# One graph network kernel: the order of the attention steps, a compare moved to ScalarE, and the zeroing of a dense table begun one stage earlier

## The chip, the core and the metric

The kernel runs on one core of one Trainium2 chip. The metric is the time on the device in microseconds (us), the median of the runs shown; lower is better. The engines of the core are TensorE (PE in the rows, PEld its weight loads), VectorE (DVE), ScalarE (ACT), GpSimd (POOL) and SyncE (SP). They run in parallel and wait for each other through semaphores. DMAs are issued from SP's and from POOL's queue and carried by 16 DMA engines.

## What is computed

A graph of 6,250 nodes with 256 features and 100,000 edges sorted by destination goes through an attention layer and then through three SAGE layers:

```
h = relu(layernorm(x));  feat = h @ W_n                    # 6250 x 256, 8 heads of 32
el, er = feat . attn_l, feat . attn_r                      # 6250 x 8 x 4 kinds
e = sum over kinds of (el[src] + er[dst] + e_pro @ attn_m) * mask / 3
e = leaky(e);  p = exp(e - segment_max(e, dst)[dst])
x = x + segment_sum(feat[src] * p, dst) / segment_sum(p, dst)
h = relu(layernorm(x))
3 times: h = l2norm(mean over edges of relu(h @ pW + pb)[src] @ lW + lb + h @ rW), silu between
out = x + layernorm(h) * ln_w + ln_b
```

The kernel treats destinations below 1536 by a dense adjacency matrix (sources by 1536 destinations, fp32) in DRAM: it is zeroed in 49 blocks of 128 rows, and then 199 scattered writes of 128 numbers each put the edge counts in.

## The kernel before

The program is unrolled by hand and has four stages.

- `setup` loads weights and indices.
- `node_features` goes over the 49 blocks of nodes in 7 groups of 7. Per group SP loads x (L373 under `load`), DVE takes the moments and ACT normalises (`norm`), PE transposes and multiplies (`project`), DVE copies the result into `table_rows` and `right_rows`, and POOL stores them (two DMAs) and waits until they have landed before it frees the rows.
- `attention` (L1365 to L1806) goes over the edges in 112 chunks of 7 tiles of 128 edges. Everything of chunk c has its step c in each engine's own order.
- `layers` are the three SAGE layers, among them the products with the dense adjacency matrix.

In `attention`, POOL gathers the 7 tiles of rows of chunk c (`gather_chunk`, 7 indirect DMAs, L499) into a ring of 5 chunks, once the sums of chunk c-5 are done (`summed`); from chunk BUILD_FROM = 54 on it adds BUILD_EACH = 4 of the scattered writes (`place_edges`, L508) behind each chunk's gathers until all 199 are out. SP loads the edges 5 chunks ahead, stores the window sums and, in steps 1 to 49, issues one block of the zeroing (L1501).

PE in step c: `left_of(c+1)` (L1535), `sum_tiles(c-1)` for tiles 0 to 3 (L1565), `to_heads(c)` (L1545 to L1548), `kinds_of(c+2)` (L1523 and 14 products at L1528), `to_edges(c)` (L1555), `sum_tiles(c-1)` for tiles 4 to 6 and the carried-over window (L1573, sets `summed`), and then a product or a transpose of a node block.

DVE in step c: `score_of(c+1)` (L1632 to L1644), `other_side(c+2)` (L1620, compares destinations with partitions and writes `one_hotT`), `run_maxima(c)` (two scans, L1652 and L1655, wait for `to_heads(c)`), every second step one of 18 pieces of counting double edges (`count_piece`, L528, L536, L539), node work (`node_norm`, `node`, `biased`), `below_max(c)` (L1663, waits for `to_edges(c)`), `shifting(c)`, and `weigh(c)` (L1678, after ACT's exponential). The 49 node blocks have slots in 49 of the steps (`slot_at`, at distances of 2 or 3); `node(n)` runs in the slot's step, `node_norm(n)` one step later, `biased(n)` four steps later.

ACT in step c: `own_side(c)` (7 absolute differences at L1775 and one relu over 128x896 at L1779), `soften(c)` (the exponentials), `normed`, `keep(c-1)` (waits for `summed`), and the node blocks' `turned` and `positive`.

## Time and profile before

| | us |
|---|---|
| median of 3 runs | 4472.72 (4471.12 to 4472.92) |
| the profiled execution | 4519.99 |
| its span, first to last instruction | 4518.3 |
| `node_features`, 60.6 to 172.9 | 112.3 |
| attention, first to last `weigh` | 1507.1 |
| `layers`, from 1772.3 | 2746.0 |

The profile is of one execution that took 1.06% longer than the median. A row of a view by groups gives line, engine, operation, output<-input, shapes and count, then busy us and mean ns of one, then the idle time of the engine just before them and what ended it. A row of the timeline gives start, length, engine, line, operation, and in brackets the idle time before it. Views by stretches give busy time and count of each engine, the granted TensorE clock (1.00 is 2.4 GHz, 0.50 is 1.2 GHz), the share of the DMA engines' time and GB/s.

### The profile page before, as it was taken

Reading aid. Unit: us, or ns where it says so; the run is one execution under the profiler, and the core shown is the slowest. Engines: PE = TensorE matmul, PEld = TensorE weight load, DVE = VectorE, ACT = ScalarE, POOL = GpSimd, SP = SyncE. Lnnn points to the kernel's source line nnn. Section 1 sums busy time; section 2 is a strip of 40 time slices with the busy share of each in tenths; the row PEclk is TensorE's granted clock in tenths of the full one; section 3 lists DMA queues with packets and bytes.
Section 4 is the critical chain, followed back from the end, with each engine's and each line's share of the span. In section 5 each row is a group of like instructions: output and inputs, shape, how many; then the busy total and the mean of one; then the engine's idle time right before and its main releaser. Section 6 shows DMA issues by size and latency. Waiting matters only on the chain.

```text
span 4518.3 us, 47445 instructions
## 1 busy us (share of the span) xinstructions
PE 3383.0 (75%) x15322; PEld 2402.7 (53%) x15322; DVE 1793.9 (40%) x5198; ACT 721.0 (16%) x2002; POOL 2672.4 (59%) x2803
## 2 busy tenths in 40 slices
PE   3477777766666676789888876898888768887875
PEld 2366556545444553456555554565555445555555
DVE  3267776544444454123232231232322313433425
ACT  1233333222222231001011110010101100000000
POOL 0355555666666653666666646666666466666663
PEclk9788889777878788799899887999999878888887
DMA  4477778544444453455555434555554345555552
GB/s 126 140 227 227 235 238 251 150 126 126 127 126 126 126 152 117 149 172 170 172 168 176 137 118 141 173 174 169 175 166 147 104 151 178 186 178 170 179 161 79
DMA packets 435311, 724.66 MB, mean 160 GB/s; under 512 B 110349, under 2 KB 260309, under 8 KB 435060
## 3 DMA queue, kind: packets, MB, share of 16 engines
q0 software_dynamic: 132272, 362.86, 28.4%
q1 hardware_dynamic: 300880, 356.54, 24.4%
q8 instruction: 124, 2.03, 0.2%
q10 hardware_dynamic: 1908, 2.19, 0.1%
q14 instruction: 127, 1.04, 0.1%
HBM read 626.59 MB, written 94.70 MB: 160 GB/s over the span
## 4 chain that ended last, share of the span: by engine, by line
PE 39%; issue 10%; another core or an unknown queue 6%; DVE 5%; ACT 0%; DMA 0%; SPq 0%; DVEq 0%
PE ps L1191 17%; PE ps L1132 16%; PE ps L1167 3%; PE ps L1157 2%; DVE attention_work L1223 1%; DVE block_cube L699 1%; DVE block_inv_norm L701 1%; DVE block_o L1254 1%; PE ps L593 0%; DVE attention_work L1245 0%; DVE root L1246 0%; DVE block_inv_norm L696 0%; DVE block_half L693 0%; DVE block_bn L651 0%
## 5 line engine op out<-in xcount | busy, mean ns | idle before, releaser
L1068 POOL DMA_INDIRECT ring<-message_table,src_index x1797 | 1704.6, 949 | 1058.9 <-issue 497.7
L1191 PE MATMUL ps<-attention_work,ring 128*128 128x128 f32 (+1 forms) x7188 | 1055.5, 295 | 392.8 <-issue 390.2
L1191 PEld LDWEIGHTS ps<-attention_work,ring 128*128 128x128 f32 x7188 | 980.5, 202 | 515.2 <-issue 493.6
L499 POOL DMA_INDIRECT ring<-attention_table,src_index x784 | 756.4, 965 | 529.1 <-issue 207.3
L1132 PE MATMUL ps<-attention_work 128*128 128x512 f32 x1764 | 856.0, 627 | 66.2 <-issue 40.1
L1565 PE MATMUL ps<-ring,one_hot 128*128 128x265 f32 x1568 | 544.7, 502 | 417.7 <-issue 417.7
L1565 PEld LDWEIGHTS ps<-ring,one_hot 128*128 128x128 f32 x1568 | 362.0, 244 | 530.7 <-issue 452.6
L1132 PEld LDWEIGHTS ps<-attention_work 128*128 128x128 f32 x1764 | 349.1, 204 | 492.1 <-issue 465.6
L1254 DVE SCALAR_TENSOR_TENSOR block_o<-ps,inv_deg,root 128x256 f32<-128x256 f32 x147 | 71.0, 483 | 872.6 <-remote 738.8
L1223 DVE TENSOR_TENSOR attention_work<-ps,attention_work 128x1024 f32<-128x1024 f32 (+1 forms) x225 | 273.4, 1216 | 361.7 <-DMA attention_work<-run_flags 359.9
L1235 DVE TENSOR_TENSOR block_aT<-ps,attention_work 128x256 f32<-128x256 f32 x111 | 47.1, 424 | 517.9 <-DMA attention_work<-run_flags 350.2
L1167 PE MATMUL ps<-w_pr,block_hT 128*128 128x512 f32 x392 | 231.7, 714 | 16.0 <-issue 14.1
L1775 ACT ACTIVATE one_hot<-iota_row,dst_rel 128x128 f32<-128x128 f32 x784 | 240.1, 391 | 19.3 <-PEq L146 19.3
L508 POOL DMA_INDIRECT dense_adjacency<-times,cell x199 | 197.0, 990 | 60.6 <-issue 60.6
L1678 DVE TENSOR_TENSOR ring<-ring,ps 128x1792 f32<-128x1792 f32 x112 | 226.4, 2022 | 3.1 <-ACT ps L1764 0.3
L1528 PEld LDWEIGHTS ps<-attention_work 128*128 128x128 f32 x1568 | 205.8, 202 | 2.1 <-DVE attention_work L1620 0.7
L1764 ACT ACTIVATE ps<-attention_work 128x56 f32<-128x56 f32 x112 | 24.8, 221 | 1079.2 <-DVE attention_work L1663 1050.8
L1528 PE MATMUL ps<-attention_work 128*128 128x32 f32 x1568 | 194.7, 278 | 0.1
L1652 DVE TENSOR_TENSOR_SCAN ps<-attention_work,ps 56x224 f32<-56x224 f32 x112 | 69.5, 621 | 264.5 <-PE ps L1548 125.0
L1348 ACT ACTIVATE attention_work<-block_o,block_shift,block_inv_norm 128x256 f32<-128x256 f32 x49 | 29.5, 601 | 840.2 <-DVE block_shift L1280 511.0
L1663 DVE TENSOR_TENSOR attention_work<-attention_work,ps 128x56 f32<-128x56 f32 x112 | 23.8, 212 | 332.6 <-DMA edge_keys<-ring 323.7
L1325 ACT ACTIVATE block_hT<-ps 128x256 f32<-128x256 f32 x98 | 37.7, 384 | 712.7 <-remote 376.6
(165 smaller groups left out, 3012.3 us busy)
## 6 DMA issues: line engine op xcount, KB each, us to landing
attention_work<-dense_adjacency SPq DMA_DIRECT2D x441, 256.0 KB
attention_work<-message_table SPq DMA_DIRECT2D x441, 128.0 KB
attention_work<-in_dst_edges SPq DMA_DIRECT2D x112, 448.0 KB
dense_adjacency<-root SPq DMA_DIRECT2D x49, 768.0 KB
ring<-message_table,src_index POOLq DMA_INDIRECT x1797
attention_sums<-sums_out SPq DMA_DIRECT2D x112, 132.5 KB
ring<-attention_table,src_index POOLq DMA_INDIRECT x784
message_table<-attention_work SPq DMA_DIRECT2D x98, 128.0 KB
```

The costliest lines, as they stand in the source:

```text
L499: pool.indirect_dma_start(m.ring[:, k, t, 0:cols], None, table, bass.IndirectOffsetOnAxis(ap=m.src[:, at:at + 1], axis=0)).then_inc(s[f"ro ...
L508: pool.indirect_dma_start(cells, bass.IndirectOffsetOnAxis(ap=m.cell[:, j:j + 1], axis=0), m.times[:, j:j + 1], None, bounds_check=BLOCKS ...
L1068: pool.indirect_dma_start(m.wide_ring[:, k, j, :], None, m.tables[w.l], bass.IndirectOffsetOnAxis(ap=m.src[:, t:t + 1], axis=0)).then_inc( ...
L1132: last = nc.tensor.matmul(m.ps[:, 2 + half, :], m.m_rows[:, k, half * P:(half + 1) * P], m.a_rows[:, k, :], start=(j == 0), stop=(j == BLO ...
L1167: last = nc.tensor.matmul(m.ps[:, 5, :], m.b_hT[:, k * P:(k + 1) * P], m.w_pr[:, w.l + 1, k, :], start=(k == 0), stop=(k == 1))
L1191: last = nc.tensor.matmul(group_sums(m, w.bank(g), (q % 2 * WIDTH + j) * PITCH, cols)[:, k, :], m.wide_ring[:, u % RING, j, k * P:(k + 1) ...
L1223: nc.vector.tensor_tensor(hot, m.iota_ps[:, None, :].to_broadcast([P, len(tiles), P]), m.dst_at[:, tiles[0]:tiles[-1] + 1][:, ::-1][:, :, ...
L1254: nc.vector.scalar_tensor_tensor(m.b_o[:], m.ps[:, 0, 0:D], m.inv_deg[:, n:n + 1], m.root[:, n, :], ALU.mult, ALU.add).then_inc(s["o"].sem, 1)
L1528: last = nc.tensor.matmul(m.ps[:, 0, t * 32:(t + 1) * 32], m.one_hotT[:, t * P:(t + 1) * P], m.right[:, k, :], start=False, stop=False)
L1565: last = nc.tensor.matmul(m.ps[:, 6 + parity, 0:SUMC], m.one_hot[:, parity, t, :], m.ring[:, k, t, 0:SUMC], start=(t == 0), stop=(c == 0 a ...
L1678: nc.vector.tensor_tensor(ring_heads[k][:, :, :, 0:HD], ring_heads[k][:, :, :, 0:HD], weights[:, :, :, None].to_broadcast([P, TILES, HEADS ...
L1775: last = nc.scalar.activation(m.one_hot[:, c % 2, t, :], m.iota_row[:], ACT.Abs, bias=m.dst_rel[:, at:at + 1], scale=-1.0)
```

## The change

- PE: the sums of chunk c-1 are split in three: tiles 0 and 1 before `to_heads(c)`, tiles 2 to 4 between `to_heads(c)` and `to_edges(c)`, tiles 5 and 6 after `kinds_of(c+2)`, which itself moves behind `to_edges(c)`.
- `other_side` moves from DVE (one compare) to ACT (an absolute difference and a relu, each over 128x896), ahead of `own_side` in the step.
- DVE: the counting pieces run in steps 1 to 18, one in each, before `run_maxima`; `node` and `node_norm` are cut in four parts, of which two go before `run_maxima`, one after it, and one (the moments) between `below_max` and `weigh`.
- Zeroing: 28 of the 49 blocks are issued in `node_features`, four behind each group's load of x on SP's queue, and the stage ends only when they have landed; the other 21 go out in attention steps 0 to 20.
- POOL: the 199 scattered writes are spread evenly behind the gathers of chunks 23 to 111 (2 or 3 each) instead of 4 behind each from 54 on.

```diff
-BEFORE = 4
-COUNT_FROM = 2
+COUNT_FROM = 1
-ZERO_FROM, BUILD_FROM, BUILD_EACH = 1, 54, 4
+ZERO_EACH = 4
+ZERO_HEAD = ZERO_EACH * GROUPS
+BUILD_FROM = 23
+def zero_block(eng, m, rows):
+    rows = rows.rearrange("o p n -> (o p) n") if len(rows.shape) == 3 else rows
+    return eng.dma_start(rows.rearrange("p (k n) -> p k n", n=ZEROS),
+                         m.zero_rows[:, None, :].to_broadcast([P, DENSE // ZEROS, ZEROS]))
@@ node_features, sync: load
                 group_dma(sp, x_g, g, m.x_in[:, b]).then_inc(s[f"x{b}"], 16)
+                if isinstance(g, int):
+                    sp.wait_ge(s["zeros"].sem, 1)
+                for k in range(ZERO_EACH):
+                    zero_block(sp, m, m.adj_groups[bass.ds(g, 1), k]).then_inc(s["zeroed"], 16)
             groups(sp, load, lambda g, b: None)
+            sp.wait_ge(s["zeroed"], 16 * ZERO_HEAD)
@@ attention, gpsimd
-                if c >= BUILD_FROM and placed < OWN:
+                if c >= BUILD_FROM:
                     if not placed:
                         pool.wait_ge(s["counted"].sem, COUNTED + 2)
-                        pool.wait_ge(s["zeroed"], 16 * BLOCKS)
-                    last = min(OWN, placed + BUILD_EACH)
+                        pool.wait_ge(s["zeroed"], 16 * (BLOCKS - ZERO_HEAD))
+                    last = OWN * (c + 1 - BUILD_FROM) // (CHUNKS - BUILD_FROM)
                     place_edges(pool, m, s, range(placed, last))
@@ attention, tensor
-                    sum_tiles(c - 1, range(BEFORE))
+                    sum_tiles(c - 1, range(2))
                 if c < CHUNKS:
                     to_heads(c)
+                if 0 < c <= CHUNKS:
+                    sum_tiles(c - 1, range(2, 5))
+                if c < CHUNKS:
+                    to_edges(c)
                 if c + 2 < CHUNKS:
                     kinds_of(c + 2)
-                if c < CHUNKS:
-                    to_edges(c)
                 if 0 < c <= CHUNKS:
-                    sum_tiles(c - 1, range(BEFORE, TILES))
+                    sum_tiles(c - 1, range(5, TILES))
@@ attention, vector, the step
                     score_of(c + 1)
-                if c + 2 < CHUNKS:
-                    other_side(c + 2)
+                if COUNT_FROM <= c < COUNT_FROM + 3 * RUN_PARTS:
+                    count_piece(nc, dve, m, s, c - COUNT_FROM)
+                elif c == COUNT_FROM + 3 * RUN_PARTS:
+                    place_cells(nc, dve, m, s)
+                for n in at_step(c, 1):
+                    node_scale(n)
+                for n in at_step(c, 0):
+                    node_weights(n)
                 if c < CHUNKS:
                     run_maxima(c)
-                if c >= COUNT_FROM and (c - COUNT_FROM) % 2 == 0:
...
-                for n in at_step(c, 1):
-                    node_norm(n)
                 for n in at_step(c, 0):
-                    node(n)
+                    node_sum(n)
...
                     biased(n)
                 if c < CHUNKS:
                     below_max(c)
                     if c:
                         shifting(c)
+                for n in at_step(c, 0):
+                    node_moments(n)
+                if c < CHUNKS:
                     weigh(c)
@@ attention, scalar
+            def other_side(c):
+                edges_in(act, c)
+                if c:
+                    act.wait_ge(s["right"].sem, s["right"].done(c - 1))
+                nc.scalar.activation(m.one_hotT, m.dst_bc[:, c % EDGES, :], ACT.Abs, bias=m.window_p[:, c:c + 1],
+                                     scale=-1.0).then_inc(s["distance"].sem, 1)
+                act.wait_ge(s["distance"].sem, s["distance"].done(c))
+                nc.scalar.activation(m.one_hotT, m.one_hotT, ACT.Relu, bias=1.0, scale=-1.0).then_inc(s["oht"].sem, 1)
+            other_side(0)
+            other_side(1)
             for c in range(steps):
+                if c + 2 < CHUNKS:
+                    other_side(c + 2)
                 if c < CHUNKS:
                     own_side(c)
```

## Rows read from the trace of the kernel before

**Rows 1.** The page: busy time of each engine, and the clock in 40 slices.
```profile
PE 3383.0 (75%) x15322; PEld 2402.7 (53%) x15322; DVE 1793.9 (40%) x5198; ACT 721.0 (16%) x2002; POOL 2672.4 (59%) x2803
PEclk9788889777878788799899887999999878888887
```

**Rows 2.** Stretches: length, then PE, PEld, DVE, ACT, POOL, clock, DMA share, GB/s.
```profile
60.60:172.90 112.30, 74.56 (x294) 52.67 (x294) 53.73 (x260) 39.79 (x64) 13.42 (x14) 0.91 0.41 131
690.90:811.30 120.40, 95.72 (x481) 73.73 (x481) 80.24 (x207) 46.02 (x137) 72.97 (x78) 0.94 0.83 254
811.30:1618.50 807.20, 515.75 (x2178) 391.75 (x2178) 373.00 (x988) 206.18 (x616) 531.66 (x550) 0.79 0.46 126
```

**Rows 3.** Stretches counted by L1678 alone, one per chunk: length, busy (count).
```profile
240.20:449.00 208.80, 36.39 (x18) 0.88 0.77 234
449.00:690.80 241.80, 40.43 (x20) 0.86 0.77 235
690.80:811.20 120.40, 22.24 (x11) 0.94 0.83 254
811.20:1618.40 807.20, 101.08 (x50) 0.79 0.46 126
```

**Rows 4.** Timeline of POOL, the end of one chunk and the next.
```profile
1033.09 0.97 POOL L508 DMA_INDIRECT dense_adjacency<-times,cell  x1 [0.31 <-issue]
1034.37 0.97 POOL L508 DMA_INDIRECT dense_adjacency<-times,cell  x1 [0.30 <-issue]
1037.79 0.98 POOL L499 DMA_INDIRECT ring<-attention_table,src_index  x1 [2.45 <-remote]
```

**Rows 5.** Timeline of PE and DVE in the same chunk.
```profile
1031.19 0.27 PE L1555 MATMUL ps<-ident,attention_work 56*128 56x56 f32 x1
1032.83 0.61 PE L1573 MATMUL ps<-sums_out,shift_mat 128*128 128x265 f32 x2
1037.45 0.21 DVE L1663 TENSOR_TENSOR attention_work<-attention_work,ps 128x56 f32<-128x56 f32 x1 [4.63 <-DMA edge_keys<-ring]
```

**Rows 6.** Timeline of POOL at the gathers' starts of chunks 9, 23 and 111.
```profile
283.73 0.94 POOL L499 DMA_INDIRECT ring<-attention_table,src_index  x1 [1.97 <-PE ps L1573]
...
448.91 0.95 POOL L499 DMA_INDIRECT ring<-attention_table,src_index  x1 [2.26 <-PE ps L1573]
...
1699.77 0.94 POOL L499 DMA_INDIRECT ring<-attention_table,src_index  x1 [1.94 <-remote]
```

**Rows 7.** DVE's groups from 240.2 to 690.8, 38 chunks.
```profile
L1620 DVE TENSOR_TENSOR attention_work<-attention_work,ps 128x896 f32<-128x896 int32 x38 | 40.9, 1076 | 0.0
L536 DVE TENSOR_REDUCE root<-root 128x199 f32<-128x1592 f32 x12 | 35.3, 2944 | 0.0
L1652 DVE TENSOR_TENSOR_SCAN ps<-attention_work,ps 56x224 f32<-56x224 f32 x38 | 23.6, 621 | 84.0 <-PE ps L1548 40.3 <-issue 25.6 <-remote 18.0
L528 DVE TENSOR_TENSOR root<-keys 128x1976 f32<-128x1976 f32 x6 | 13.1, 2182 | 0.0
L539 DVE TENSOR_TENSOR root<-root 128x199 f32<-128x199 f32 x10 | 3.7, 367 | 0.3
```

**Rows 8.** ACT's group of the relu, same stretch.
```profile
L1779 ACT ACTIVATE one_hot<-one_hot 128x896 f32<-128x896 f32 x38 | 36.2, 951 | 1.2
```

**Rows 9.** DMA in 40 slices of 0.65 us, two groups of `node_features`, 101 to 127.
```profile
DMA  0008999960000949991000099999500005599900
GB/s 0 0 0 321 357 357 270 353 151 0 0 0 6 54 147 373 388 384 60 0 0 0 0 350 372 350 262 349 126 0 0 0 24 106 165 386 388 318 25 0
```

**Rows 10.** GB/s in 40 slices, 253 to 258, a zeroing block issued at 253.76.
```profile
GB/s 344 258 201 401 267 305 362 257 249 202 319 302 400 253 393 374 284 250 231 226 164 244 111 240 348 381 349 393 393 442 377 393 410 377 442 377 431 398 387 333
```

**Rows 11.** Timeline, the first counting piece beside a gather.
```profile
246.10 2.18 DVE L528 TENSOR_TENSOR root<-keys 128x1976 f32<-128x1976 f32 x1
246.48 2.63 POOL L499 DMA_INDIRECT ring<-attention_table,src_index  x1 [0.30 <-issue]
```

41 lines of the change are left out of this document (14 added, 27 removed).

## The prediction, made before the changed kernel had run

> **What bounds the kernel now.** I read the page first. No engine is busy throughout: PE has 75%, POOL 59%, DVE 40%, ACT 16% [rows 1]. So the question is which chain sets the pace in each stage, and the view by stretches comes next. The change touches `node_features` (112.3 us, DMA share 0.41) and the attention [rows 2]; `layers` is neither shortened nor fed with other data, and I carry its 2746 us over unchanged.
>
> Inside the attention one DVE instruction, `weigh` at L1678, marks each chunk. Counting it by stretches gives the pace [rows 3]: 208.8 / 18 = 11.60 us per chunk at first, 241.8 / 20 = 12.09 after that, 120.4 / 11 = 10.95 where the counting pieces are over, and 807.2 / 50 = 16.14 in the stretch where POOL adds four scattered writes per chunk. The reader is to see that half of the attention's time lies in the last figure, and that PE, DVE and ACT are all idler there (PE 515.8 of 807.2 us, clock down to 0.79) than in the stretch before it (95.7 of 120.4, clock 0.94) [rows 2]. Something on POOL's side sets the pace.
>
> POOL's timeline shows what: each indirect DMA takes 0.95 to 1.0 us and the next starts 0.30 us later, and between two chunks there is a gap, here 2.45 us [rows 4]. A gather is thus worth 1.25 us and a scattered write 1.28; 7 x 1.25 + 4 x 1.29 = 13.9 us, and 16.14 - 13.9 leaves 2.2 us for the gap. Without the writes the same gap is 1.9 to 2.3 [rows 6], so POOL's floor for a bare chunk is 7 x 1.25 + 2.0 = 10.8 us, just under the 10.95 of [rows 3]. **POOL's queue is the floor of both kinds of chunk.** The gap is odd: the semaphore it waits for was set by L1573 at 1033.4, and DVE's L1663 stood 4.6 us although L1555 had ended at 1031.5 [rows 5]. Both go on about 2 us after POOL's last DMA. I cannot say from the trace what holds them; I take the gap as a price per chunk.
>
> **Part 1, the scattered writes spread.** POOL does the same 784 gathers and 199 writes. What can be gained is only the time in which it now stands still for the other engines outside the build. From the start of chunk 23's gather (448.91) to that of chunk 111 (1699.77) the kernel takes 1250.9 us [rows 6]. Afterwards all 88 intervals hold 199 / 89 = 2.24 writes on average: 16.14 - 1.76 x 1.29 = 13.86 us each, 1220 us in all. That is **-31 us**. It holds if the other engines need less than 13.5 us per chunk; they need 10.95 or less now. The lower bound takes the gap at 1.97 instead of 2.2 [rows 6]: -31 - 88 x 0.23 = -51. The upper bound lets four in ten steps, those with the most node work, run over by 0.5 us: -13.
>
> **Part 2, the counting, now in every one of steps 1 to 18.** A piece is 2.9 us of DVE ((13.1 + 35.3 + 3.7) / 18) [rows 7]. What one costs the pace now: 38 chunks took 450.6 us against 38 x 10.95 = 416, so 34.5 / 18 = 1.9 us each; the rest falls in waits. Twice the density over 18 steps gives 10.95 + 1.9 = 12.9 us per chunk. Against that `other_side` leaves DVE, 1.08 us per chunk [rows 7], and the pieces stand where DVE now waits for `to_heads`, 84.0 / 38 = 2.2 us per chunk [rows 7]. But that wait shrinks, for `to_heads` has only two tiles of sums ahead of it, and `kinds_of` now lies between `to_edges(c)` and `left_of(c+2)`, so the next score comes later. The two roughly cancel. I take 12.4, half a microsecond less than the plain sum for the compare. Against 11.60 that is 18 x 0.8 = **+14 us**. Bounds: the piece hidden whole, 11.2 (-7); not hidden at all, 13.9 (+41).
>
> **Part 3, the rest of the reordering.** Where POOL is the floor, a shorter chain on PE or DVE buys nothing, so from step 19 on I cost the new order of sums, `kinds_of` and node parts at zero. What hides it is POOL's 13.9 us per chunk. `summed` is set about 1.5 us later than before (2.1 us of `kinds_of` stand ahead of it in place of one tile and a half of sums), which POOL's wait would feel if the step were over 12 us; that is inside part 1's upper bound. ACT gets two instructions like L1779, 2 x 0.95 = 1.9 us per chunk [rows 8], on top of 46.0 / 11 = 4.2 [rows 2]. ACT now waits for `right` there, with `own_side` and `soften` queued behind it, and `weigh` waits for `soften`. 6.1 us of work in a step of 10.8 or more leaves room: 0, with 1 us at the start, where nothing covers ACT's first two. If the cover went, the price would be 1.9 us per chunk.
>
> **Part 4, zeroing in `node_features`.** A block is 786 KB, four are 3.15 MB. A group's own traffic is 0.92 MB of x and 1.18 MB of stores, in two bursts of about 3 and 4 us at 350 GB/s, with pauses between them; two groups fill 26 us [rows 9]. While a zeroing block moves, the DMA engines carry some 400 GB/s [rows 10], so four take 7.9 us. 7 + 7.9 = 14.9 us of transfers for a group that takes about 12.8 us now: the stage becomes bound by transfers once it runs. In SP's queue the load of group g+1 stands behind the four blocks of group g; POOL's stores share the engines with them, and DVE waits until the stores have landed. The first load has nothing ahead of it and the second has slack, so I count 2.1 us for six groups, **+12 us**. Bounds: +4 (only the last load is late) to +30 (each store takes 4 us longer in six groups and the loads slip too).
>
> A rule bears on this sum. The Trainium skill, DMA: Bandwidth & Descriptors, Specifications, gives the traffic between a core and its DRAM a limit of about 358 GB/s; by it a group's 5.25 MB need 14.7 us, an estimate that lands beside mine, though slices of [rows 10] show up to 442 GB/s, above that limit.
>
> **Part 5, the end.** POOL now has three writes behind its last gathers, 3.9 us, where it had none; if VectorE's wait of [rows 5] also hangs on them, the last chunks come up to 3.9 us later: +3. The 21 zeroing blocks left in the attention end at step 20, chunk 23's writes wait for them, and four chunks of ring cover that: 0, at most +5.
>
> Sum: -31 + 14 + 1 + 12 + 3 = **-1 us**; with the smaller gaps of the bare chunks half taken in, I call it -3. Against the profiled execution's 4519.99 that is 4517; its changes carry over to the median, 1.06% lower, nearly one to one, so 4472.7 - 3 = 4470.
>
> **The rivals.**
> - *The pieces vanish in DVE's wait and the zeroing in the pauses.* For it: 3.3 us per chunk of DVE time free ahead of the scans (2.2 of wait and 1.08 of compare) are more than the piece's 2.9, and the DMA share of the stage is 0.41. Against it: the wait was PE's work, which does not shrink. -7 + 4 - 31 + 3 + 1 = -30: 4443. Chance 0.30.
> - *The stores and loads of `node_features` starve* (the one on the other side). The place is the pair of SP's load behind 3.1 MB of zeros and POOL's store beside them; it decides once zeros and bursts together move at less than 330 GB/s, when a group takes 16 us and more. Then +30 in part 4 while the rest stays: +15 to +20, 4490. Chance 0.20.
> - *The step becomes the bound in the build.* `kinds_of` between `to_edges` and `left_of` lengthens the chain when the clock is at half (PE's 95.7 / 11 = 8.7 us per step were measured at 0.94, and the build has 0.79 [rows 2]), the node parts ahead of the scans add 1.9, and DVE's stall of [rows 5] ties each step to POOL's pause. It decides from 13.5 us per step. At 14.3 the 88 intervals cost 38 us more than I count: 4506. Chance 0.12.
> - *A counting piece holds POOL.* The first one lay over a gather that took 2.63 us instead of 0.95 [rows 11]. The page SBUF — State Buffer of the Trainium skill, Who interferes with whom, says that an instruction of VectorE with two inputs in SBUF contends only with GpSimd instructions that read SBUF, and infers that descriptor generation needs the write side; by that nothing would be held, and the row differs from it. The count of L528 stays six and in steps 1 to 18 POOL waits anyway, so neither gives another time here: inside the forecast.
> - *It doesn't do what it says:* chunk 23's writes wait for zeroing or counting for many steps. Chance 0.03, about 4475.
>
> **How the numbers follow.** The forecast, -18 to +15 around 4470, has 0.35. A difference below about 0.2% (9 us) can't be told from no change in this kernel. From the forecast I put 0.12 on faster by more, 0.17 on the same, 0.06 on slower; the first rival gives 0.26 faster and 0.04 same; the second 0.16 slower and 0.04 same; the third 0.12 slower; the last 0.03 same. Together 0.38, 0.28 and 0.34. For eight in ten the range goes from 4438, below the first rival, to 4504, at the third. The forecast's own range is 4455 to 4488.
>
> **What would show it.** In the new profile: `weigh` at 13.7 to 14.0 us per chunk from about chunk 24 to the end (part 1), 12 to 13 in the first 18 (part 2), `node_features` 8 to 20 us longer with its load waits ended by DMAs (part 4), an attention of 1480 to 1510 us from first to last `weigh`. The prediction is wrong if POOL's gap isn't a price per chunk but moves with the order on PE, if the first 18 chunks go at POOL's 10.8, or if the steps in the build pass 14 us.

## The result and the profile after

The changed kernel takes **4578.02 us** (4556.73 to 4590.58, four runs), the kernel before 4472.82 (4471.12 to 4477.33, four runs): a ratio of 1.022, 95% interval 1.019 to 1.025. The change costs 105 us; forecast were -3. The profiled execution took 4590.58 us, its span is 4589.1.

The page of the changed kernel, busy times and clock in 40 slices, answers to [rows 1]:

```profile
PE 3467.9 (76%) x15322; PEld 2451.6 (53%) x15322; DVE 1672.5 (36%) x5085; ACT 941.2 (21%) x2226; POOL 2671.9 (58%) x2803
PEclk9777787777787878789989887899898878899887
```

POOL has the same work, DVE 121 us less and ACT 220 us more, as forecast. PE has the same 15322 products and 85 us more for them; its granted clock is lower in the attention, in slices 3 to 7 above all.

The view by stretches answers to [rows 2], first `node_features` (length, then busy and count of PE, PEld, DVE, ACT, POOL, clock, DMA share, GB/s):

```profile
60.60:190.30 129.70, 76.47 (x294) 53.17 (x294) 53.60 (x261) 39.87 (x64) 13.39 (x14) 0.91 0.77 283
```

It is 17.4 us longer, and 283 GB/s move in it instead of 131. POOL's timeline at the gathers' starts of chunks 5, 23 and 111 answers to [rows 6]:

```profile
258.72 0.94 POOL L515 DMA_INDIRECT ring<-attention_table,src_index  x1 [23.82 <-PE ps L1578]
...
507.89 0.95 POOL L515 DMA_INDIRECT ring<-attention_table,src_index  x1 [2.66 <-PE ps L1586]
...
1781.08 0.98 POOL L515 DMA_INDIRECT ring<-attention_table,src_index  x1 [1.92 <-remote]
```

From chunk 23 to 111 that is 1273.2 us where the first trace of before has 1250.9 [rows 6] and 1220 were forecast. From 5 to 23 it is 249.2. The profiled execution of before was 1% over its median, so a second trace of it was taken later, on another chip; in it these stretches are 1233.4 and 200.9 us. I go by that one, since it took 4463.05 us, 0.2% under the median. The stretches of the changed kernel, then those of the second trace of before, chunks 5 to 23 and 23 to 111 (length, POOL's busy time, clock, DMA share, GB/s):

```profile
258.70:507.90 249.20, 126.43 (x127) 0.76 0.64 198
507.90:1781.10 1273.20, 786.53 (x813) 0.79 0.50 141
```

```profile
241.60:442.50 200.90, 124.60 (x126) 0.90 0.80 243
442.50:1675.90 1233.40, 788.37 (x815) 0.82 0.57 165
```

Where the time went, in us, from the starts of these gathers and from the first and the last `weigh` (an ordinary table; the rows of the runs are shown with them):

```
                          first     chunks      chunks      gather 111 to
                          weigh     5 to 23     23 to 111   last weigh      last weigh
before, first trace       230.1       207.4      1250.9        37.5          1737.3
before, second trace      230.3       200.9      1233.4        37.4          1713.3
changed kernel            247.5       249.2      1273.2        36.9          1818.0
difference to the second  +17.2       +48.3       +39.8        -0.5          +104.7
forecast of it            +13          +14         -31          +3             -1
```

The +104.7 us is as large as the 105.2 between the medians, but that is partly luck. The two profiled executions lie 127.6 us apart in span, and 22.9 of these are behind the last `weigh`, in a stage that the change leaves alone (2771.1 and 2748.2 us); measured against the first trace of before, the attention's loss is 80.7 us, +41.8 in chunks 5 to 23 and +22.3 in 23 to 111. So each figure of the table can be some ten or twenty us off, and the two losses are there by either trace. Part 4 came out about as forecast, and two terms did not: the first 18 steps cost 34 us more than counted, and where 31 us should be gained 40 are lost. The second of these has a pattern. The interval between the gathers' starts of two chunks is 11.4 to 15.7 us in 79 of 88, mostly 13.1 or 14.6, as forecast, but nine have 21.7 to 23.9 (chunks 26, 38, 41, 50, 54, 70, 73, 86, 102). The 79 have a mean of 13.55; nine times the excess is 81 us.

One of the nine, in the timeline of the changed kernel, the scans of chunk 98:

```profile
1638.92 0.95 POOL L515 DMA_INDIRECT ring<-attention_table,src_index  x1 [0.31 <-issue]
1639.67 0.38 PE L1561 MATMUL ps<-ident,attention_work 128*56 128x48 f32 x2
1645.17 1.02 POOL L524 DMA_INDIRECT dense_adjacency<-times,cell  x1 [0.30 <-issue]
1646.50 0.99 POOL L524 DMA_INDIRECT dense_adjacency<-times,cell  x1 [0.30 <-issue]
1650.47 0.62 DVE L1659 TENSOR_TENSOR_SCAN ps<-attention_work,ps 56x224 f32<-56x224 f32 x1 [11.05 <-remote]
```

PE's product for `to_heads` ends at 1640.05, and that is what the scan waits for (its edge data, which it waits for too, were there for the score before). VectorE, which runs its work in order, goes on at 1650.47, 3.0 us after POOL's last DMA. That is the stall of [rows 5], larger, and in another place of the step.

### The profile page after: what moved, and what is told of

Same layout as the page of the kernel before. It is cut to its first block, busy times and chain, and to the rows that moved or that the text cites. A ratio compares the mean times of both kernels' runs of the same rounds, so it can differ in the third digit from the quotient of the medians.

```text
span 4589.1 us, 47604 instructions
## 1 busy us (share of the span) xinstructions
PE 3467.9 (76%) x15322; PEld 2451.6 (53%) x15322; DVE 1672.5 (36%) x5085; ACT 941.2 (21%) x2226; POOL 2671.9 (58%) x2803
## 4 chain that ended last, share of the span: by engine, by line
PE 41%; issue 10%; another core or an unknown queue 5%; DVE 4%; ACT 0%; DMA 0%; SPq 0%; DVEq 0%
PE ps L1207 18%; PE ps L1148 16%; PE ps L1183 4%; PE ps L1173 3%; DVE block_cube L715 1%; DVE attention_work L1239 1%; DVE block_o L1270 0%; DVE block_inv_norm L717 0%; PE ps L609 0%; DVE block_bn L667 0%; DVE block_inv_norm L712 0%; DMA attention_work<-message_table 0%; DVE attention_work L1261 0%; DVE block_half L709 0%
## 5 line engine op out<-in xcount | busy, mean ns | idle before, releaser
L1207 PE MATMUL ps<-attention_work,ring 128*128 128x128 f32 (+1 forms) x7188 | 1041.9, 293 | 363.8 <-issue 361.0
L1207 PEld LDWEIGHTS ps<-attention_work,ring 128*128 128x128 f32 x7188 | 969.9, 201 | 475.7 <-issue 453.4
L1148 PEld LDWEIGHTS ps<-attention_work 128*128 128x128 f32 x1764 | 350.4, 205 | 504.2 <-issue 477.9
L1578 PE MATMUL ps<-ring,one_hot 128*128 128x265 f32 x1568 | 557.6, 497 | 14.7 <-issue 14.3
L1558 PE MATMUL ps<-ident,attention_work 128*56 128x48 f32 x224 | 38.7, 261 | 322.0 <-DVE attention_work L1643 159.4
L1639 DVE TENSOR_TENSOR attention_work<-ps,attention_work 128x224 f32<-128x224 f32 x112 | 43.9, 392 | 629.1 <-remote 391.8
L1183 PE MATMUL ps<-w_pr,block_hT 128*128 128x512 f32 x392 | 241.0, 734 | 27.8 <-issue 26.4
L1541 PEld LDWEIGHTS ps<-attention_work 128*128 128x128 f32 x1568 | 251.6, 241 | 4.6 <-issue 1.6
L1541 PE MATMUL ps<-attention_work 128*128 128x32 f32 x1568 | 238.0, 312 | 0.9 <-issue 0.9
L1558 PEld LDWEIGHTS ps<-ident,attention_work 128*56 128x56 f32 x224 | 23.3, 150 | 369.1 <-DVE attention_work L1643 180.5
L1803 ACT ACTIVATE sums_out<-ps 128x265 f32<-128x265 f32 x112 | 44.0, 393 | 683.8 <-remote 486.3
```

Source lines behind the costliest of these rows:

```text
L1148: last = nc.tensor.matmul(m.ps[:, 2 + half, :], m.m_rows[:, k, half * P:(half + 1) * P], m.a_rows[:, k, :], start=(j == 0), stop=(j == BLO ...
L1183: last = nc.tensor.matmul(m.ps[:, 5, :], m.b_hT[:, k * P:(k + 1) * P], m.w_pr[:, w.l + 1, k, :], start=(k == 0), stop=(k == 1))
L1207: last = nc.tensor.matmul(group_sums(m, w.bank(g), (q % 2 * WIDTH + j) * PITCH, cols)[:, k, :], m.wide_ring[:, u % RING, j, k * P:(k + 1) ...
L1541: last = nc.tensor.matmul(m.ps[:, 0, t * 32:(t + 1) * 32], m.one_hotT[:, t * P:(t + 1) * P], m.right[:, k, :], start=False, stop=False)
L1578: last = nc.tensor.matmul(m.ps[:, 6 + parity, 0:SUMC], m.one_hot[:, parity, t, :], m.ring[:, k, t, 0:SUMC], start=(t == 0), stop=(c == 0 a ...
```

## The experiments

Experiments ran on several chips, and these were of two kinds. On the first kind the kernel before takes 4463 to 4482 us, as in the first measurement; on the second 3858 to 3871. Which kind a kernel met was chance, so a ratio is always that to the kernel before on the same chip. "Kind of chip" is a name for what was met: the chip with number 4 shows 4470.8 us beside the experiments of section 2 and 3859.8 us beside `h_start_two`, so either the number doesn't stand for the same chip both times or one chip can be of either kind. What the second kind does differently became the main finding.

### 1. One edit alone, on a chip of the second kind

Two theories stood against each other: the new order on PE costs the time (O), or the spread writes do (B). `a_pe_old` is the changed kernel with PE's old order (the `if` lines are left out here):

```diff
-                    sum_tiles(c - 1, range(2))
+                    sum_tiles(c - 1, range(4))
                 to_heads(c)
-                    sum_tiles(c - 1, range(2, 5))
-                to_edges(c)
                 kinds_of(c + 2)
+                to_edges(c)
-                    sum_tiles(c - 1, range(5, TILES))
+                    sum_tiles(c - 1, range(4, TILES))
```

> The changed kernel with the old order on PE alone: four tiles of sums, to_heads, kinds_of, to_edges, three tiles of sums. Theory O (order): the new order on PE sets summed and the input of the next score later, so that a step now and then misses POOL's pause and waits for a whole further run of POOL's (the ten steps of 22 to 28 us, 9 to 10 us too much each), and lengthens the first 18 steps. It expects these long steps gone and 80 to 110 us less than the changed kernel, 4470 to 4500 us. Theory B (build): the writes spread over 88 chunks cause the long steps whatever PE's order: within 20 us of the changed kernel's 4578.

`a_build_old` is the changed kernel with the writes as before:

```diff
-BUILD_FROM = 23
+BUILD_FROM, BUILD_EACH = 54, 4
...
-                if c >= BUILD_FROM:
+                if c >= BUILD_FROM and placed < OWN:
...
-                    last = OWN * (c + 1 - BUILD_FROM) // (CHUNKS - BUILD_FROM)
+                    last = min(OWN, placed + BUILD_EACH)
```

> The changed kernel with the scattered writes as before, four behind each chunk from 54 on, all else new. Theory O expects long steps in the stretch without writes too and no gain of more than 20 us, 4560 to 4600. Theory B expects the long steps gone between chunks 23 and 54, and that 31 us of forecast gain were never there: 4500 to 4540.

`b_pe_new` is the kernel before with the new order on PE (the diff of `a_pe_old`, reversed). `b_zero_new` is the kernel before with `ZERO_EACH = 4` blocks per group in `node_features` and 21 in steps 0 to 20.

> The kernel before with the new order on PE and nothing else. Theory O: slower by 40 to 100 us, 4510 to 4570, with steps of over 20 us. Theory B: within 10 us of the kernel before, 4463 to 4483, since POOL's queue is the floor and covers PE.

> The kernel before with 28 of the 49 zeroing blocks in node_features and the other 21 in steps 0 to 20, and nothing else. The two traces have the first weigh 17.4 us later after the change. If all of that is the zeroing: +15 to +20 for node_features, less what the attention's first 49 steps gain when fewer blocks cross them (0 to 10): 4478 to 4493. If most of it is the rest (the compare on ScalarE before the first score, the order on PE): 4470 to 4480.

Then the changed kernel itself and the kernel before, for their traces there:

> The changed kernel itself, unedited. The first four experiments ran on a chip on which the kernel before takes 3861 us, not 4473; there the pauses of 2 us between POOL's chunks are missing (gathers of chunks start 8.8 us apart, 14.0 with four writes), and the new order on PE alone made the kernel before faster by 25 us. Theory W (late wake-ups): the loss of the changed kernel comes from the late ends of waits that the first chip shows and this one doesn't; then the changed kernel is no slower than the kernel before on such a chip: 3820 to 3855 us, and 4560 to 4590 on a chip like the first. Theory C (cost in the kernel itself): slower by 1 to 2.5% on either: 3900 to 3960, or 4520 to 4590.

> The kernel before, unedited, for its trace on the chip of the experiments. Theory W: where the kernel takes some 3860 us, VectorE's wait for the transposed maxima in the stretch of the four writes per chunk ends within 0.3 us of PE's product, and chunks' gathers start 8.8 and 14.0 us apart; where it takes some 4470 us, both show the pauses of about 2 us. Theory C: pauses on both.

Measured, with the kernel before at 3861 us beside the four edited kernels and at 3871 beside `before_again` and `after_again`:

```
              ratio to before, 95% interval     us       first weigh   5 to 23   23 to 111
before_again  (one run)                         3868.1      203.0       182.6     1070.0
after_again   1.0084  1.0061 to 1.0106          3899.2      215.7       227.7     1041.7
a_pe_old      0.9966  0.9955 to 0.9977          3848.2      217.0       179.0     1038.3
a_build_old   1.0075  1.0058 to 1.0092          3889.2      216.7       228.0     1038.1
b_pe_new      0.9933  0.9917 to 0.9950          3835.7      202.9       167.3     1059.5
b_zero_new    1.0037  1.0025 to 1.0050          3875.2      216.6       182.3     1076.6
```

Here the changed kernel loses 0.8%, not 2.2%, and its 3899.2 us lie between the ranges of theories W and C. O and B are each right in part. Chunks 23 to 111 gain 28 us, close to the 31 of part 1, and no interval is over 17.5 us: the loss of the build belongs to the first kind of chip. The first 18 steps lose 45 us here too, so this loss is in the kernel. The old order on PE takes it away whole (227.7 to 179.0), and yet the new order alone makes the kernel before faster, by 15 us in these same steps. Neither order is bad; the new one is bad together with something else that the change brings. The zeroing in `node_features` moves the first `weigh` by 13.6 us and the time by 14. The writes spread or not make no difference in this setting (1041.7 and 1038.1): what the changed kernel gains after chunk 23 doesn't come from the spreading. With the writes as before, its chunks 23 to 54 start 8.9 us apart (`a_build_old`), where the kernel before needs 10.0 (`before_again`).

### 2. What goes on in the first 18 steps

The timeline of the changed kernel on the second kind of chip, PE and DVE in one of these steps:

```profile
415.30 2.91 PE L1541 MATMUL ps<-attention_work 128*128 128x32 f32 x14
418.02 2.11 PE L1578 MATMUL ps<-ring,one_hot 128*128 128x265 f32 x4
420.81 2.60 PE L1601 MATMUL ps<-w_pr,block_hT 128*128 128x512 f32 x4
423.25 0.54 PE L1548 MATMUL ps<-ring,ident 128*128 128x224 f32 x2
423.90 0.39 DVE L1639 TENSOR_TENSOR attention_work<-ps,attention_work 128x224 f32<-128x224 f32 x1 [6.45 <-PE ps L1548]
424.89 2.96 DVE L552 TENSOR_REDUCE root<-root 128x199 f32<-128x1592 f32 x1
428.17 0.61 DVE L1659 TENSOR_TENSOR_SCAN ps<-attention_work,ps 56x224 f32<-56x224 f32 x1
429.39 0.27 PE L1568 MATMUL ps<-ident,attention_work 56*128 56x56 f32 x1 [2.21 <-DVE attention_work L1662]
```

PE does `kinds_of` (L1541), the last sums, a node block's product (L1601) and then `left_of` (L1548), and VectorE stands 6.45 us for that. Then VectorE does the score, the counting piece (L552) and the scans, and PE stands 2.21 us for these before `to_edges` (L1568), behind which `kinds_of` comes again. The two engines take turns. In the old order `kinds_of` stood ahead of `to_edges` and ran under the counting piece. Theory K says that this is the loss: one chain through both engines, closed by two edits, `kinds_of` behind `to_edges` and a piece ahead of the scans. Two kernels cut it in different places, a third builds it into the kernel before. The fourth is an attempt at a better one.

`a_kinds_early`, the changed kernel with one swap:

```diff
-                if c < CHUNKS:
-                    to_edges(c)
                 if c + 2 < CHUNKS:
                     kinds_of(c + 2)
+                if c < CHUNKS:
+                    to_edges(c)
```

> The changed kernel with kinds_of(c+2) back ahead of to_edges(c); the sums stay split two, three, two. Theory K (one chain): in steps 1 to 18 the new place of kinds_of ties PE and VectorE into one chain, scans, to_edges, kinds_of, sums, left_of, score, counting piece, scans, with PE idle under the piece and VectorE idle under kinds_of. It expects nearly all of the 50 us that the old order gave to be back, 3845 to 3865 where the kernel before takes 3865, and the gather of chunk 23 at 412 to 425 instead of 462. Theory S (split): it is the sums that now stand on both sides of to_edges: 3885 to 3900. On a chip like the first: K 4480 to 4520, S 4560 to 4590.

`a_count_late`, the changed kernel with `count_piece` behind `run_maxima`:

> The changed kernel with each counting piece behind the two scans of its step instead of ahead of them. Theory K: the piece then lies beside kinds_of on PE and leaves the chain, though it now holds back below_max and weigh: 20 to 40 us less than the changed kernel's 3899, 3860 to 3880, gather of chunk 23 at 425 to 440. Theory L (load): VectorE has simply more to do in each of these steps than the step holds, wherever the piece stands: 3890 to 3905.

`b_pe_count`, the kernel before with the new order on PE and a piece in each of steps 1 to 18 ahead of the scans:

> The kernel before with the new order on PE and one counting piece in every step 1 to 18, ahead of the scans; all else as before. The new order alone gave 25 us less, and the piece in every step cost nothing with the old order (the changed kernel with it reaches chunk 23's gather 12 us later than the kernel before, and starts 16 us later). Theory K: the two together cost what neither does, gather of chunk 23 at 425 to 445 against 400, 3880 to 3900. Theory A (ScalarE): the loss needs the compare on ScalarE or the node parts ahead of the scans, and this kernel keeps the gain of 25: 3835 to 3850.

`h_mix`, the changed kernel with PE's old order, `ZERO_EACH = 2` and `BUILD_FROM = 38`:

> An attempt to beat both: the changed kernel with the old order on PE, 14 blocks of the zeroing in node_features instead of 28 (two per group, the other 35 in steps 0 to 34), and the writes spread over chunks 38 to 111 instead of 23 to 111. Theory K: the old order gives back 51 us, two blocks per group fit into the pauses of the transfers and give back 5 to 10 of the 14 that the zeroing cost alone, and POOL's queue still sets the pace behind chunk 38: 3835 to 3845. If the zeroing costs in the attention what it saves in node_features: 3845 to 3855.

These four fell on a chip of the first kind, with the kernel before at 4470.8 us:

```
               ratio to before, 95% interval    us       first weigh   5 to 23   23 to 111
a_kinds_early  0.9985  0.9974 to 0.9996         4464.3      246.3       204.5     1201.8
a_count_late   1.0076  1.0059 to 1.0094         4508.9      244.7       197.6     1271.7
b_pe_count     1.0073  1.0055 to 1.0091         4503.7      227.7       235.8     1236.9
h_mix          0.9996  0.9981 to 1.0011         4469.9      234.6       216.7     1211.1
```

The stretches of the first two, chunks 5 to 23 and 23 to 111 (length, POOL's busy time, clock, DMA share, GB/s), `a_kinds_early` first:

```profile
257.00:461.50 204.50, 125.75 (x126) 0.88 0.78 240
461.50:1663.30 1201.80, 790.87 (x812) 0.84 0.54 150
```

```profile
255.80:453.40 197.60, 128.97 (x126) 0.87 0.80 248
453.40:1725.10 1271.70, 786.21 (x812) 0.76 0.50 142
```

For the first 18 steps theory K holds on each cut: 249.2 us becomes 204.5 with `kinds_of` early and 197.6 with the piece behind the scans, and `b_pe_count`, which has only the two edits, loses 35 us against the 200.9 of before. The compare on ScalarE and the node parts aren't needed for the loss, and the split of the sums (theory S), which `a_kinds_early` keeps, isn't its cause. (Its build has four long intervals of 22.0 to 25.6 us, which it makes up in the bare steps from 23 to 54, 10.7 us each against 11.5.) The granted clock differs with it: 0.88 and 0.87 in the two cuts, 0.76 in the changed kernel in these steps. `kinds_of`'s 14 products took 2.91 us at 415.30 above, at a granted clock of 0.52 and after PE had stood 2.91 us for the scans, and 1.65 us in the next step, at 1.00. So the ring's link on PE is longer where the clock is at its lower level; how much of the 45 to 50 us that makes wasn't measured.

The other half is new. `a_count_late` cures the first 18 steps and keeps the whole loss of the build: 1271.7 us, nine intervals of over 20 us again. `a_kinds_early` has none of them and takes 1201.8. So one swap is worth 71 us in a stretch where no counting goes on, PE has over a quarter of the time free, and POOL is the floor. The swap brings the kernel from 1.022 to 0.9985.

Against `a_kinds_early`, `h_mix` gives back 12 us at the start and needs 12 more in chunks 5 to 23 and 9 more in the build. On this kind of chip it is no better than the kernel before; its expectation of 3835 to 3845 us was for the other kind, where it didn't run. `a_kinds_early` came out under theory K's 4480 to 4520 by 16 us.

### 3. Late wake-ups

The groups of DVE from chunk 23 to 111 tell what the swap moves (last column: idle time before it, and what ended it). The changed kernel:

```profile
L1659 DVE TENSOR_TENSOR_SCAN ps<-attention_work,ps 56x224 f32<-56x224 f32 x88 | 54.6, 620 | 107.8 <-remote 80.6 <-PE ps L1561 23.8 <-issue 3.4
L1639 DVE TENSOR_TENSOR attention_work<-ps,attention_work 128x224 f32<-128x224 f32 x89 | 34.9, 392 | 494.1 <-remote 350.6 <-PE ps L1548 115.3 <-issue 28.2
L1670 DVE TENSOR_TENSOR attention_work<-attention_work,ps 128x56 f32<-128x56 f32 x88 | 18.6, 212 | 71.4 <-issue 41.0 <-PE ps L1568 16.4 <-remote 13.9
```

`a_kinds_early`:

```profile
L1659 DVE TENSOR_TENSOR_SCAN ps<-attention_work,ps 56x224 f32<-56x224 f32 x88 | 54.6, 621 | 60.7 <-issue 54.2 <-PE ps L1561 6.5
L1639 DVE TENSOR_TENSOR attention_work<-ps,attention_work 128x224 f32<-128x224 f32 x88 | 33.8, 384 | 2.5 <-remote 2.5
L1670 DVE TENSOR_TENSOR attention_work<-attention_work,ps 128x56 f32<-128x56 f32 x88 | 18.9, 214 | 548.8 <-remote 545.5 <-PE ps L1568 3.2
```

VectorE stands for these three 673 us in the changed kernel and 612 with `kinds_of` early. With `kinds_of` early it stands at the wait for `to_edges` (L1670), as before the change. In the changed kernel it stands at the wait for `left_of` (L1639), and now and then at the scans (L1659).

To see what holds a wait I took, from the timelines, each case in which VectorE was idle until one of these three instructions, and set the delay between the end of PE's product and VectorE's start against POOL: in which DMA of an unbroken run (gaps under 0.6 us), counted from its start, the product ended. Of idle times under 0.3 us none is counted; other limits move the counts by some ten, not the picture.

```
                                        waits ended over 1 us late
                                 product ended early in the run   product ended late in the run
changed kernel, first kind       DMA 1 to 5:    4 of 140          DMA 6 and later:   80 of 82
before, second trace, first kind DMA 1 to 3:    0 of 11           DMA 7 and later:   56 of 58
changed kernel, second kind      DMA 1 to 5:    0 of 20           DMA 6 and later:    0 of 178
before, second kind              DMA 1 to 5:    0 of 15           DMA 6 and later:    0 of 133
```

On the first kind of chip a signal that PE sends in the first DMAs of POOL's run reaches VectorE after 0.1 us. One that it sends after about the sixth reaches it when the run is over, mostly 1.6 to 2.4 us after the last DMA. What is late is the signal and not VectorE: the trace records the semaphore's own update 0.1 us or less before VectorE goes on (86 of 90 late waits of the changed kernel), which is why the views above put these waits down to "remote" and not to PE. (In DMAs 4 to 6 of the kernel before it goes either way, 25 of 105 late.) On the second kind no signal is late, in runs of up to 815 DMAs. POOL's own wait for `summed` has the same delay, which is the pause of 2 us between chunks; there the gathers' starts are 8.8 us apart, and 14.0 with four writes.

So each chunk has one held wait, and it matters which. If it is the one for `to_edges`, the whole rest of the step, up to the scans of the next chunk, fits into POOL's pause and the first DMAs of the next run: in the build of `a_kinds_early` the wait of L1670 is late in 88 of 88 chunks, that of the scans in none. If it is the one for `left_of`, the score, `to_heads` and the scans come after it, and when one of them comes later than usual, the signal for the scans falls behind the fifth DMA as well and waits for a further run, and the chunk takes 9 us longer. In the changed kernel L1639's wait is late 68 times, the scans' 9 times, and there are nine long intervals. But the place in the run isn't the whole rule. In three of the nine the product for the scans had ended in the third or fourth DMA of a run already, here in chunk 37:

```profile
759.50 0.38 PE L1561 MATMUL ps<-ident,attention_work 128*56 128x48 f32 x2
759.52 0.94 POOL L515 DMA_INDIRECT ring<-attention_table,src_index  x1 [0.31 <-issue]
765.84 0.99 POOL L524 DMA_INDIRECT dense_adjacency<-times,cell  x1 [0.31 <-issue]
769.03 0.62 DVE L1659 TENSOR_TENSOR_SCAN ps<-attention_work,ps 56x224 f32<-56x224 f32 x1 [8.37 <-remote]
```

These three are three of the 4 of 140. What makes just these nine steps late is open.

The direct test breaks POOL's run. `a_pause` is the changed kernel with two writes of POOL between the fourth and fifth gather of each chunk (its definitions of the buffer and the semaphore are left out here); `before_slow` is the kernel before, for its second trace:

```diff
+PAUSE = 1024
...
+        if t == 4 and cols == ROW:
+            for r in range(2):
+                if c or r:
+                    pool.wait_ge(s["paused"].sem, 2 * c + r)
+                nc.gpsimd.iota(m.pause[:], [[1, PAUSE]], base=0, channel_multiplier=0,
+                               allow_small_or_imprecise_dtypes=True).then_inc(s["paused"].sem, 1)
         pool.indirect_dma_start(m.ring[:, k, t, 0:cols], None, table,
```

> The kernel before, unedited, for a second trace. If the first trace, 1% over its median, was long in the attention: on a chip like the first the last weigh comes near 1711 instead of 1737 us, with shorter bare steps. If it was long in the layers: last weigh at 1735 to 1740 and the layers 25 to 45 us shorter than 2781. On a chip of the other kind: last weigh at 1501, as in the second trace there.

> The changed kernel with two writes of 128x1024 by POOL between the fourth and fifth gather of each chunk, a pause in its run of DMAs of 2 to 3 us; it computes nothing that is used. Theory R (run): on a chip like the first, waits of idle engines end only once POOL's indirect DMAs stop. Then they end in the pause as well, the ten steps of 22 to 28 us become 15 to 17, and what POOL loses in the pause it gains at the chunk's end, where summed has been set: 4480 to 4570. Theory N (nothing to do with it): the long steps stay and the pauses add up, 112 x 2.5 = 280 us: 4700 to 4860. On a chip of the other kind only the pauses can be seen: 4000 to 4180.

Both met a chip of the second kind (before at 3857.6 us). `a_pause` took 4069.2 us there, ratio 1.056 (1.053 to 1.058): where no wait is held, the pauses cost 170 us against the changed kernel's 3899.2, 1.5 us a chunk, near the 1.9 that they take from POOL. `before_slow` had its last `weigh` at 1493.6. The same two kernels again:

> The kernel before, unedited, for its trace. On a chip like the first: if the first trace was long in the attention, the last weigh comes near 1711 instead of 1737 us; if in the layers, near 1737 with layers of 2735 to 2755 instead of 2781. On a chip of the other kind: 1501, as before.

> The changed kernel with the two writes by POOL between the fourth and fifth gather once more. On a chip of the other kind they took 2.05 us a chunk and cost 170 us in all, 1.5 us a chunk; there it will be 4060 to 4080 again. On a chip like the first: theory R (the run of DMAs holds the waits) expects that waits of idle engines end in the pause too, no steps of over 20 us, 4480 to 4600; theory N expects the long steps to stay and 170 to 210 us to be added, 4740 to 4790.

This time the chip was of the first kind. The same kernel took **4469.5 us** (one run; two of the kernel before on the same chip took 4463.1 and 4482.4), 108 us less than the changed kernel without the pauses, which ran on another chip of that kind. That is just below theory R's 4480 to 4600 and far from theory N's 4740 to 4790: added work of 2.05 us per chunk on the engine that is the floor made it faster. Its timeline, around the last two DMAs of a run:

```profile
599.15 0.26 PE L1568 MATMUL ps<-ident,attention_work 128*56 128x48 f32 x2
600.09 0.95 POOL L522 DMA_INDIRECT ring<-attention_table,src_index  x1 [0.30 <-issue]
601.06 2.05 POOL L520 IOTA pause<- 128x1024 f32 x2
602.85 0.62 DVE L1666 TENSOR_TENSOR_SCAN ps<-attention_work,ps 56x224 f32<-56x224 f32 x1 [2.26 <-remote]
603.26 0.95 POOL L522 DMA_INDIRECT ring<-attention_table,src_index  x1 [0.15 <-issue]
```

PE's product ends at 599.41, POOL's last DMA at 601.04, and the scan starts 1.8 us after that, inside the pause. No interval of chunks 23 to 111 is over 15 us. The stretches, 5 to 23 and 23 to 111:

```profile
243.40:471.80 228.40, 161.59 (x163) 0.79 0.70 211
471.80:1677.80 1206.00, 963.68 (x988) 0.81 0.53 149
```

The build takes 1206.0 us, 67 less than the changed kernel's 1273.2, as with the swap. `a_pause` on the second kind of chip has the same stretch:

```profile
475.10:1680.20 1205.10, 962.17 (x988) 0.85 0.55 150
```

Without the pauses the two kinds are 231 us apart there (1273.2 and 1041.7), with them 1; its first 18 steps take 227.0 and 228.4 us, and its last `weigh` comes at 1709.8 and 1706.6. The pauses at the chunks' ends are gone, since `summed` is there when POOL comes to it: 7 gathers, 2 or 3 writes and the pause make 13.4 or 14.7 us. The first `weigh` comes at 220.4 instead of 247.5 us, because the first 35 gathers are one run and hold a wait too: in the second trace of before VectorE stands 33.8 us for chunk 1's scores, until 28.9 us after PE's product. The first 18 steps keep most of their loss (228.4), as theory K says. That the unbroken run of DMAs holds the waits, theory R, is shown, and with it what they cost in the build; by what mechanism it holds them is not.

`before_third` gave the second trace: 4463.05 us, last `weigh` at 1713.3, and 2748.2 us behind it where the first trace had 2781.0. The first trace was longer in both parts, by 24 and 33 us.

### 4. Kernels built on it

`h_steps` is the changed kernel with `kinds_of` behind `to_edges` only in the bare steps 19 to 49, no zeroing in `node_features`, and the writes as before:

```diff
+                bare = COUNT_FROM + 3 * RUN_PARTS <= c < BUILD_FROM - RING + 1
+                if c + 2 < CHUNKS and not bare:
+                    kinds_of(c + 2)
                 if c < CHUNKS:
                     to_edges(c)
-                if c + 2 < CHUNKS:
+                if c + 2 < CHUNKS and bare:
                     kinds_of(c + 2)
```

> An attempt to beat both. The changed kernel with kinds_of ahead of to_edges in steps 1 to 18 and from 50 on, and behind it only in the bare steps 19 to 49; no zeroing in node_features (49 blocks in steps 0 to 48) and the writes as before, four behind each chunk from 54 on. The start goes back by 16 us, the first 18 steps are as with kinds_of early, the bare steps go at POOL's 10.4 to 10.8 instead of 11.9 (31 x 1.2 = 37 us), the build at 16.1 as before. On a chip like the first 4430 to 4450; on the other kind 3830 to 3845 (against 3865).

> The changed kernel with kinds_of ahead of to_edges once more. Theory K: on a chip like the first again within 0.3% of the kernel before, 4455 to 4475; on a chip of the other kind 3845 to 3865 against 3865, gather of chunk 23 at 410 to 425. Theory S (the split of the sums matters there): 3880 to 3900.

`h_start` is `h_steps` with the pause in chunks 2, 3 and 4 alone; `h_start_two` is the same kernel.

> h_steps with POOL's pause of two writes in chunks 2, 3 and 4 alone, between the fourth and fifth gather. In the third trace of before (chip like the first) VectorE waits 33.8 us for the scores of chunk 1, until POOL's first 35 gathers are out, though PE's product ended at 194.5. Theory R: on a chip like the first the pause at 196 lets it go on, the first weigh comes at 203 to 208 instead of 230 us, the bare steps 19 to 49 go at 10.4 to 10.8 (new order there), the build at 16.0: last weigh at 1650 to 1670 instead of 1713, the median 4420 to 4445 against 4471. On a chip of the other kind nothing is held; the pauses can cost up to 6 us there: 3830 to 3845 against 3858.

> The same kernel once more. Theory R: on a chip like the first the first weigh comes at 203 to 208 instead of 230 us, the last at 1650 to 1670 instead of 1713, the median at 4420 to 4445 against 4471. If the start gained goes into POOL's pace later (the ring full, the build at 16.0 whatever comes before), less: 4445 to 4465. On a chip of the other kind again 3835 to 3850 against 3858.

All four ran on chips of the second kind (before at 3858 to 3860 us):

```
              ratio to before, 95% interval     us       first weigh   5 to 23   23 to 111
a_kinds_two   0.9958  0.9943 to 0.9973          3840.4      220.0       173.0     1040.7
h_steps       0.9935  0.9916 to 0.9954          3832.6      203.8       176.9     1053.6
h_start       0.9947  0.9929 to 0.9964          3840.1      205.0       182.8     1051.2
h_start_two   0.9941  0.9927 to 0.9954          3837.4      205.2       175.7     1049.1
```

`h_steps` beats both kernels on the second kind, by 25 us against before and by some 60 against the changed kernel (3899.2), no more than `b_pe_new` did with one edit (0.9933). The three pauses cost about nothing there. Whether `h_start` reaches its 4420 to 4445 us on the first kind wasn't measured. There `a_kinds_early` is the best that ran with an interval, at 0.9985, and that is within what can't be told from no change.

`a_kinds_two`, the swap on the second kind, also shows the missing chain (its 3840.4 us are under theory K's 3845 to 3865): VectorE's idle time ahead of L1639 in chunks 5 to 23 is 66.5 us in the changed kernel and 13.5 with `kinds_of` early, first and second fence:

```profile
L1639 DVE TENSOR_TENSOR attention_work<-ps,attention_work 128x224 f32<-128x224 f32 x17 | 6.7, 392 | 66.5 <-PE ps L1548 66.5
```

```profile
L1639 DVE TENSOR_TENSOR attention_work<-ps,attention_work 128x224 f32<-128x224 f32 x17 | 6.6, 388 | 13.5 <-PE ps L1548 13.5
```

The 53 us between them are nearly all of the 54.7 by which the stretch differs (227.7 and 173.0).

## Why the prediction was wrong, step by step

- **What bounds the kernel: right, with its riddle left unread.** POOL's queue is the floor. The prediction noted that `summed` was set long before POOL went on and that L1663 stood 4.6 us although PE had finished [rows 4, 5], said that it couldn't tell what holds them, and went on with "I take the gap as a price per chunk". For the gap that was good enough: in `a_kinds_early` the 106 intervals from chunk 5 to 111 hold 742 gathers and 196 writes, 742 x 1.25 + 196 x 1.29 = 1180 us, and take 1406, so 2.1 us each. But the same effect also holds VectorE, and there its price depends on where in POOL's run a signal falls. A look at whether PE's product at 1031.19 fell early or late in the run, and at how the same wait fared in other chunks, would have shown most of the rule in the trace of before.
- **Part 1, the writes spread: -31 forecast.** With `kinds_of` early the stretch takes 1201.8 us against 1233.4, **-31.6**; in the changed kernel it is +39.8. That -31.6 meets the -31 is in part luck: the forecast was 1220 from the first trace's 1250.9, and 1201.8 is 49 below that. Nor is it shown to be the spreading. No run on the first kind undoes the spreading alone, on the second it was worth nothing (1041.7 and 1038.1), and the counting pieces and the compare, which leave VectorE in these chunks, are in the same stretch. The condition that the prediction put, other engines under 13.5 us per chunk, was met in 79 of 88 intervals as far as their length tells (13.55 us on average); nine took a second run of POOL.
- **Part 2, the counting: +14 forecast, +48.3 measured.** This is a failed step. "The two roughly cancel" weighed the place of `kinds_of` against the shorter way to `to_heads`. It named the link, `kinds_of` between `to_edges(c)` and `left_of(c+2)`, but did not walk round the ring: scans, `to_edges`, `kinds_of`, sums, `left_of`, score, piece, scans. With `kinds_of` early it is +3.6, with the piece late -3.3; so the piece in every step costs next to nothing by itself. The +48.3 lies above my upper bound of +41, which was the piece not hidden at all (by the first trace it is +41.8): a ring can cost more than the work that is put into it, since PE's part no longer hides either.
- **Part 3, the rest of the reordering: 0 forecast, +71 in the build.** The other failed step: "where POOL is the floor, a shorter chain on PE or DVE buys nothing", and so a changed order costs nothing. It cost 71 us on the first kind of chip (1273.2 against 1201.8, and 1271.7 in `a_count_late`, which ran on the same chip as `a_kinds_early`) and 1 us on the second (1041.7 against 1040.7). Cover by POOL's 13.9 us holds for work, not for a signal that POOL's run holds back. ScalarE's 1.9 us per chunk were hidden as forecast: `a_kinds_early` has them too.
- **Part 4, the zeroing: +12 and +1 at the start forecast, +17.2 measured,** within its bounds. The group of DVE's copies in `node_features` waits 36.6 us for POOL's stores instead of 20.2, and that of the moments 9.0 us for x instead of 2.8: both waits grow, the one for the stores by 16 us and the one for the loads by 6, in the place that the rival on starving named, though short of its 30 us. The stage moved 283 GB/s on average, so its transfers weren't the bound throughout; my sum had transfers alone and no wait for the stores behind the zeros. The limit of the Trainium skill (DMA: Bandwidth & Descriptors, Specifications), 358 GB/s, wasn't reached on average either, and doesn't decide here.
- **Part 5, the end: +3 forecast,** -0.5 in the changed kernel, +3.7 in `a_kinds_early`.
- **The rivals.** "The step becomes the bound in the build" had the right place and both ingredients, `kinds_of` between `to_edges` and `left_of` and the stall of [rows 5], but as 88 steps of 14.3 us, at 38 us in all and a chance of 0.12. It came as nine steps of 22 us, and the chain in the counting came on top. The first rival's piece that vanishes in the waits is what the piece does once `kinds_of` is early. The rival on a piece that holds POOL was right to change nothing: in the changed kernel five gathers beside L544, the former L528, take 2.0 to 3.0 us instead of 0.95, and the first 18 steps are long for the other reason.
- **What would show it.** `weigh` at 13.7 to 14.0 us per chunk was nearly so (13.55 without the nine), 12 to 13 in the first 18 was not (13.8), and the attention took 1570 us from first to last `weigh` instead of 1480 to 1510. The point named as fatal, that POOL's gap "moves with the order on PE", is what happened, to the hold on VectorE rather than to the gap itself.
- **The sum.** With the measured terms: 17.2 + 48.3 + 39.8 - 0.5 = 104.7 (rounded), against medians 105.2 apart. With `kinds_of` early: 16.0 + 3.6 - 31.6 + 3.7 = -8.3, against -6.5 by the medians on its chip. Both sums leave out what lies behind the last `weigh`, 22.9 and 14.5 us more than in the second trace of before, so that they meet the medians so closely is luck. The -3 was near for the change without one of its edits, but with +14 for what was +3.6 and with a gain that may not be the spreading's.

## What to carry to other kernels

When two engines each wait for the other in a step, walk round the whole ring of waits in the new order before an edit is costed at nothing, and put what nobody waits for soon (`kinds_of`) under the other engine's long piece. When a wait in a trace ends long after what it waits for, don't book it as a price: list every such case against what another engine was doing at that time, because an edit will move the next signal into or out of it. And take a second trace when the profiled execution lies outside the kernel's own runs.

## What the runs showed of the hardware

- On one kind of chip, a semaphore signal of PE sent in about the sixth indirect DMA of an unbroken run of POOL or later reached the waiting VectorE mostly 1.6 to 2.4 us after the run's last DMA (80 of 82 in the changed kernel, up to 13 us late, and 29 us in the first run of 35); of those sent earlier 136 of 140 took under 1 us, mostly 0.1. A break of 2 us in the run, with POOL busy on its own writes, lets the signals through. On the other kind of chip none of 311 was late, and the same kernel before takes 3861 instead of 4471 us. What differs isn't settled, nor whether it belongs to the chip, since chip number 4 shows both; nor was it tried how short a break may be.
- Part of the distance between the kinds is in the other stage: behind the last `weigh` the kernel before takes 2748.2 and 2365.7 us, with granted clocks of 0.89 and 0.95. How much of that is held waits and how much clock was not measured.
- PE's granted clock was lower where PE stood in a ring of waits, on both kinds: 0.76 and 0.79 in the changed kernel's chunks 5 to 23, 0.88 and 0.95 with `kinds_of` early.
- A gather of POOL beside a VectorE instruction with two inputs in SBUF (L528, 128x1976, 2.18 us) took 2.5 to 3.3 us instead of 0.95, five times in the first trace of before.
